# A perceiver layer on one core: products of zeros before the first rows, the identity inside x, the query weights in four pieces

## The chip, the cores and the metric

One core of a Trainium2 chip runs the whole layer in one launch. The metric is the device time of one execution in microseconds (us). The engines of the core are TensorE (PE: matmuls and transposes, with its weight loads as PEld), VectorE (DVE), ScalarE (ACT), GpSimd (POOL) and SyncE (SP), which issues every load and store. Each works through its own list of instructions in order; they wait for each other on semaphores.

## What is computed

The reference is one layer on x of 256 tokens by 512, in float32: cross-attention over 4096 context rows and the layer's own 256, then latent attention of 16 heads with rotary positions and a causal mask, then a mixture of 32 experts with one shared expert. Only the first lines matter for the change:

```python
x = x + xattn(layernorm(x), ctx_2048, ctx_2048, wq, wk, wv, wo)
# inside xattn:
q = einsum('bsd,ed->bse', x, wq)
k_new = einsum('bsd,ed->bse', x, wk)
k = concatenate([k_cache, k_new]); v = concatenate([v_cache, v_new])
attn = softmax(einsum('bqd,bkd->bqk', q, k) / sqrt(512))
out = einsum('bqk,bkd->bqd', attn, v) @ wo.T
x = x + latent_attention(layernorm(x), ...)
x = x + experts(layernorm(x), ...)
```

## The kernel before

**Precision.** Every product is made of three matmuls: each operand is split into a high part rounded to `fp32r` and a low part that holds the rest, and `product` (L375) issues high*high, low*high (or high*low) and the other cross term (L377, L380, L381). ScalarE makes the high part of a weight tile (`split_hi`, L269) and VectorE the low part (`split_lo`, L276). A result in a PSUM bank is split in the same way on its way out: `out_hi`, `out_lo` (L284, L288) and, for transposed tokens, `tokens_hi`, `tokens_lo` (L315, L319).

**Weight tiles.** Weights and context come through two slots of `raw`, `w_hi`, `w_lo`, used in turn. A tile of the first part of the kernel is 128 partitions by 2048 floats, 1 MB, in two halves of 512 KB. A half covers two chunks of 128 rows of the contraction (`x_chunk`). `load` (L330) issues both halves; except for the first two tiles it waits until the tile before in the same slot has been split (`lo_split`). The tiles follow each other: query weights (T_WQ), key weights (T_WK), eight context tiles (T_CT), value weights, eight context tiles again, and so on.

**The start, engine by engine.** SP issues (L338 to L344): the two halves of x (128 tokens each, 256 KB, into `res`), the identity (the first 128 columns of `small`, read as 128 rows of 512 B), the query weights in two halves, the rest of `small` (mask, rotary tables, router weights, gains: 640 KB), the key weights in two halves, the rope weights. VectorE takes the statistics of each half of x, GpSimd the power -0.5 (`root`), VectorE normalizes to `xn`. TensorE waits for the identity (L441), transposes `xn`, half 0 into banks 0 and 1 and half 1 into banks 4 and 5, and then runs `project_t` (L404) twice: for each of four blocks m of output features it goes through all four chunks c of the contraction. Query results fill banks 2 and 3, key results banks 4 and 5. Then come the score groups (`score_group`, L448), each on one context tile: 24 matmuls with 512 columns.

ScalarE's list at the start (L846 to L866): high part of query half 0, the four evictions of transposed tokens, query half 1, key halves 0 and 1, two query evictions, the halves of the first context tile, two key evictions, then the constants (`ident_r`, two blocks of `mask_r`, `rw_hi`), two blocks of rope weights, and then the loop over context tiles from the second one on. VectorE (L1109 to L1130) makes the low parts in the same order.

`mask_r` has three blocks of 128 columns. Block 0 is all zeros, set by GpSimd (`mask_zeroed`); it is part of the causal mask that enters the scores of the latent attention in the middle of the kernel.

Of the kernel before, what the change touches and what calls it, by code (L numbers as in the profile page):

```python
# [29 lines left out]
F32 = mybir.dt.float32  # L30
# [5 lines left out]
P = 128  # L36
# [34 lines left out]
C_ID, C_MASK, C_COS, C_SIN, C_RW, C_BIAS, C_GQ, C_GKV, C_TIE = 0, 128, 256, 512, 768, 896, 960, 1152, 1280  # L71
# [39 lines left out]
def perceiver_layer(nc, x, small, wq, wk, wv, wo, ctx_t, ctx_n, w_qkv, w_rope, w_mla, w_exp, out):  # L111
    with ExitStack() as ctx:
# [12 lines left out]
        res = sb("res", [P, 2, D])  # L125
# [92 lines left out]
        ident_loaded = sem("ident_loaded")  # L218
# [64 lines left out]

        def out_hi(act, b, full, hi, n, rows=slice(0, P), at=0, scale=1.0):  # L284
            act.wait_ge(bank_full[b], full)
            act.activation(hi, bank[b][rows, at:at + n], ACT.Copy, scale=scale).then_inc(ev_hi, 1)  # L286
# [42 lines left out]
        def _(sp):  # L329
# [8 lines left out]
            for h in range(2):  # L338
                sp.dma_start(res[:, h, :], x[:, h, :]).then_inc(x_loaded[h], 16)
            sp.dma_start(smalls[:, C_ID:C_MASK], small[:, C_ID:C_MASK]).then_inc(ident_loaded, 16)  # L340
            load(Tile(0, T_WQ), wq, X_SIZES, first=True)
            sp.dma_start(smalls[:, C_MASK:C_END], small[:, C_MASK:C_END]).then_inc(small_loaded, 16)
            load(Tile(0, T_WK), wk, X_SIZES, first=True)
            sp.dma_start(probs[0:QR2].rearrange("p a b c -> p (a b c)"), w_rope[0:QR2, :]).then_inc(rope_w_loaded, 16)  # L344
# [27 lines left out]
        def _(pe):  # L372
            ident = smalls[:, C_ID:C_ID + P]
# [67 lines left out]
            pe.wait_ge(ident_loaded, 16)  # L441
            for h in range(2):
                transpose_half(xn, h, 4 * h, xn_ready, h + 1)
            project_t(Tile(0, T_WQ), 2, split=V_LN1 + 2)
# [145 lines left out]
            pe.wait_ge(mask_zeroed, 1)  # L590
# [254 lines left out]
        def _(act):  # L845
            split_hi(act, Tile(0, T_WQ), 0, X_SIZES, first=True)  # L846
            for h in range(2):
                tokens_hi(act, 4 * h, (F01 if h == 0 else F45)["ln1"], xt_hi, h)
            split_hi(act, Tile(0, T_WQ), 1, X_SIZES, first=True)
# [8 lines left out]
            act.wait_ge(ident_loaded, 16)  # L858
            act.copy(ident_r[:, :], smalls[:, C_ID:C_ID + P]).then_inc(consts_rounded, 1)
# [212 lines left out]
        def _(dve):  # L1072
# [41 lines left out]
            split_lo(dve, Tile(0, T_WQ), 0, X_SIZES)  # L1114
            for h in range(2):
                tokens_lo(dve, 4 * h, V_LN1 + 2 * h, xt_hi, xt_lo, h)
            split_lo(dve, Tile(0, T_WQ), 1, X_SIZES)
# [414 lines left out]
        def _(pool):  # L1532
# [5 lines left out]

            pool.memset(power[:, :], -0.5).then_inc(power_set, 1)
            pool.memset(mask_r.bitcast(F32)[:, 0, :], 0.0).then_inc(mask_zeroed, 1)  # L1540
# [91 lines left out]
```

## Time and profile before

| | |
|---|---|
| median of 3 runs | 560.92 us (560.76 to 561.14) |
| the profiled execution, its own time | 559.95 us |
| its span, first to last instruction | 558.2 us |
| TensorE busy | 534.0 us, 96% |
| VectorE busy | 392.9 us, 70% |
| ScalarE busy | 314.0 us, 56% |
| mean granted TensorE clock | 0.997 |
| DMA | 86.43 MB, mean 155 GB/s |

All times in the rows are microseconds from the start of the span. Busy shares are averages over stages with different limits; a stage is read by the wait that ends last in it. A name such as L279 is the line of the helper that issued the instruction, so one line stands for many places: the time and the tile tell them apart.

### The profile page before, as it was taken

What the parts mean: (1) busy time and instruction counts of PE and PEld (TensorE: products, weight loads), DVE (VectorE), ACT (ScalarE), POOL (GpSimd) and SP (SyncE); (2) the same over time, 40 slices, a digit from 0 to 9 for tenths busy, and PEclk for the clock granted to TensorE, in tenths of its full rate; (3) what the DMA queues carried; (4) which work ended last, traced back from release to release, by engine and by line L of the source; (5) the groups of instructions that cost most, each with busy time, mean ns of one, the idle gap of its engine ahead of it and who ended that gap; (6) DMA issues with size and microseconds to landing.
All of it is one profiled execution on the core that took longest, in us unless ns stands there. A gap on an engine that the chain in (4) does not pass through costs nothing.

```text
span 558.2 us, 9698 instructions
## 1 busy us (share of the span) xinstructions
PE 534.0 (96%) x3448; PEld 478.8 (86%) x3448; DVE 392.9 (70%) x597; ACT 314.0 (56%) x506; POOL 5.4 (1%) x14
## 2 busy tenths in 40 slices
PE   3999999999888999998999999999999999999997
PEld 3978888888778888877889999999999999999996
DVE  4686655557877777677587767767767777677675
ACT  3666476753566676765645464564654655645631
POOL 1000000000100000000000000000000000000000
PEclk9999999999998999999999999999999999999999
DMA  8855534445132222440636456455465464564621
GB/s 263 256 179 200 175 128 136 161 155 170 38 113 77 77 75 75 128 174 11 228 114 225 155 183 210 149 205 188 155 220 170 168 220 149 195 205 144 215 66 39
DMA packets 19138, 86.43 MB, mean 155 GB/s; under 512 B 2128, under 2 KB 2256, under 8 KB 19024
## 3 DMA queue, kind: packets, MB, share of 16 engines
q1 hardware_dynamic: 19120, 86.19, 46.4%
q8 instruction: 11, 0.18, 0.1%
q14 instruction: 7, 0.06, 0.0%
HBM read 85.66 MB, written 0.52 MB: 154 GB/s over the span
## 4 chain that ended last, share of the span: by engine, by line
PE 80%; DVE 8%; ACT 7%; issue 2%; DMA 1%; SPq 0%; ACTq 0%; POOL 0%; DVEq 0%
PE bank L377 26%; PE bank L381 26%; PE bank L380 26%; ACT scores L960 2%; DVE w_lo L279 2%; ACT scores L969 2%; ACT w_hi L274 1%; DVE m_neg L1299 1%; PE bank L486 1%; DMA raw<-wq_dram 1%; ACT operands L286 1%; DVE operands L290 1%; PE bank L640 1%; DVE res L1449 1%; DVE rope_w L1129 0%
## 5 line engine op out<-in xcount | busy, mean ns | idle before, releaser
L274 ACT CAST w_hi<-raw 128x1024 fp32r<-128x1024 f32 (+1 forms) x160 | 161.7, 1044 | 138.6 <-PE bank L377 122.0
L279 DVE TENSOR_TENSOR w_lo<-raw,w_hi 128x1024 fp32r<-128x1024 f32 (+1 forms) x160 | 187.9, 1215 | 12.2 <-ACT w_hi L274 10.3
L377 PE MATMUL bank<-xt_hi,w_hi 128*128 128x256 f32 x544 | 155.2, 285 | 2.9 <-DVE xt_lo L311 2.9
L380 PE MATMUL bank<-xt_lo,w_hi 128*128 128x256 f32 x544 | 154.6, 284 | 0.0
L381 PE MATMUL bank<-xt_hi,w_lo 128*128 128x256 f32 x544 | 154.5, 284 | 0.0
L377 PE MATMUL bank<-w_hi,operands 128*128 128x512 f32 (+1 forms) x320 | 126.4, 395 | 3.1 <-DVE operands L311 1.4
L381 PE MATMUL bank<-w_hi,operands 128*128 128x512 f32 (+1 forms) x320 | 124.5, 389 | 0.0
L380 PE MATMUL bank<-w_lo,operands 128*128 128x512 f32 (+1 forms) x320 | 124.5, 389 | 0.0
L377 PEld LDWEIGHTS bank<-xt_hi,w_hi 128*128 128x128 f32 x544 | 104.9, 193 | 4.8 <-issue 3.3
L380 PEld LDWEIGHTS bank<-xt_lo,w_hi 128*128 128x128 f32 x544 | 105.0, 193 | 1.5
L381 PEld LDWEIGHTS bank<-xt_hi,w_lo 128*128 128x128 f32 x544 | 105.0, 193 | 0.0
L377 PEld LDWEIGHTS bank<-w_hi,operands 128*128 128x128 f32 x320 | 60.2, 188 | 15.5 <-DVE operands L311 1.8
L1449 DVE SCALAR_TENSOR_TENSOR res<-bank,weights,res 128x512 f32<-128x512 f32 x68 | 50.8, 750 | 30.0 <-PE bank L381 30.0
L381 PEld LDWEIGHTS bank<-w_hi,operands 128*128 128x128 f32 x320 | 60.0, 187 | 13.8
L380 PEld LDWEIGHTS bank<-w_lo,operands 128*128 128x128 f32 x320 | 60.1, 188 | 11.1
L290 DVE TENSOR_TENSOR operands<-bank,operands 128x512 fp32r<-128x512 f32 (+2 forms) x81 | 47.4, 626 | 28.8 <-ACT operands L286 28.7
L286 ACT ACTIVATE operands<-bank 128x512 fp32r<-128x512 f32 (+2 forms) x81 | 40.3, 560 | 32.6 <-PE bank L381 17.3
L1511 DVE TENSOR_TENSOR operands<-scores,operands 128x512 fp32r<-128x512 f32 x32 | 22.2, 693 | 41.1 <-ACT operands L1058 41.1
L377 PE MATMUL bank<-operands 128*128 128x256 f32 (+2 forms) x110 | 31.4, 285 | 1.8 <-DVE operands L290 1.8
L381 PE MATMUL bank<-operands 128*128 128x256 f32 (+2 forms) x110 | 31.7, 288 | 0.0
L380 PE MATMUL bank<-operands 128*128 128x256 f32 (+2 forms) x110 | 31.7, 288 | 0.0
L377 PEld LDWEIGHTS bank<-operands 128*128 128x128 f32 x110 | 21.6, 196 | 5.2 <-DVE operands L290 5.0
(152 smaller groups left out, 503.2 us busy)
## 6 DMA issues: line engine op xcount, KB each, us to landing
raw<-w_exp_dram SPq DMA_DIRECT2D x34, 896.0 KB, 4.8
raw<-w_exp_dram SPq DMA_DIRECT2D x34, 640.0 KB, 5.6
raw<-ctx_t_dram SPq DMA_DIRECT2D x16, 512.0 KB, 4.4
raw<-ctx_n_dram SPq DMA_DIRECT2D x16, 512.0 KB, 3.8
raw<-w_mla_dram SPq DMA_DIRECT2D x16, 512.0 KB, 4.2
raw<-wq_dram SPq DMA_DIRECT2D x2, 512.0 KB, 6.4
raw<-wk_dram SPq DMA_DIRECT2D x2, 512.0 KB, 11.5
raw<-wv_dram SPq DMA_DIRECT2D x2, 512.0 KB, 4.6
```

Of the source, the lines that this page charges most:

```text
L274: act.copy(w_hi[:, t.slot, at:at + n], raw[:, t.slot, at:at + n]).then_inc(hi_split[k], 1)
L279: eng.tensor_tensor(w_lo[:, t.slot, at:at + n], raw[:, t.slot, at:at + n], w_hi[:, t.slot, at:at + n].bitcast(F32), ALU.subtract) \
L286: act.activation(hi, bank[b][rows, at:at + n], ACT.Copy, scale=scale).then_inc(ev_hi, 1)
L290: dve.tensor_tensor(lo, bank[b][rows, at:at + n], hi.bitcast(F32), ALU.subtract) \
L377: ins = pe.matmul(o, a[0], b[0], start=start, stop=False)
L380: pe.matmul(o, a[0], b[1], start=False, stop=False)
L381: return pe.matmul(o, a[1], b[0], start=False, stop=stop)
L486: ins = pe.transpose(bank[2 * ring + h][:, k * P:k * P + P], probs[:, ring, h, k * P:k * P + P], ident)
L960: act.activation(pair_probs[:, hd, at:at + n], bank[2 + hd][:, at:at + n], ACT.Exp, bias=m_bias[:, k:k + 1], scale=q_scale[:, h:h + 1], ac ...
L969: act.activation(v, v, ACT.Copy, scale=m_inv[:, 2 * hd + h:2 * hd + h + 1]).then_inc(m_norm, 1)
L1449: dve.scalar_tensor_tensor(out=res[:, h, :], in0=bank[b][:, :], scalar=w, in1=res[:, h, :], op0=ALU.mult, op1=ALU.add).then_inc(res_done, 1)
L1511: dve.tensor_tensor(h_lo[:, s % 2, :], h_row[:, s % 2, :], h_hi[:, s % 2, :].bitcast(F32), ALU.subtract).then_inc(ev_lo, 1)
```

## The change

1. GpSimd zeroes block 0 of `mask_r` before it sets `power`. TensorE waits for that alone and issues 12 matmuls of this block with itself (128 x 128 by four repeats of the block, 512 columns) into bank 7, and one each into banks 2 and 3, which leaves zeros there. Two more follow the transposes of half 0 and four those of half 1.
2. x comes from the host as one array of 128 by 1280: half 0, identity, half 1, and 128 unused columns. The first transfer brings half 0 and the identity (rows of 2560 B, 320 KB), the second half 1 (256 KB). `res` and `ident` are views of `first_rows`. `small` loses its identity columns and is loaded whole, behind the key weights.
3. The query weights come in four transfers of 256 KB, one for each chunk, with a semaphore each, and are split chunk by chunk (`wq_hi`, `wq_lo`). ScalarE rounds chunk 0 and chunk 1 before the evictions of half 0 and half 1 of the tokens, VectorE takes chunk 0 before the tokens and chunks 1 to 3 after them.
4. `project_q` turns the two loops of `project_t` around: for each chunk c all four blocks m. All results accumulate onto the zeros in banks 2 and 3 (`start=False`).

```diff
-        res = sb("res", [P, 2, D])
+        first_rows = sb("first_rows", [P, 2 * (D + P)])
+        res = first_rows[:, :].rearrange("p (h n) -> p h n", h=2)[:, :, 0:D]
+        ident = first_rows[:, D:D + P]
...
+        def wq_hi(act, c):
+            k, at = c // 2, OFF[c // 2] + (c % 2) * 512
+            act.wait_ge((loaded_b if k else loaded_a)[0] if c % 2 else wq_loaded[k], 16)
+            act.copy(w_hi[:, 0, at:at + 512], raw[:, 0, at:at + 512]) \
+               .then_inc(hi_split[k] if c % 2 else wq_hi_split, 1)
+
+        def wq_lo(dve, c):
+            k, at = c // 2, OFF[c // 2] + (c % 2) * 512
+            if c % 2:
+                dve.wait_ge(hi_split[k], 1)
+            else:
+                dve.wait_ge(wq_hi_split, k + 1)
+            dve.tensor_tensor(w_lo[:, 0, at:at + 512], raw[:, 0, at:at + 512],
+                              w_hi[:, 0, at:at + 512].bitcast(F32), ALU.subtract) \
+               .then_inc(lo_split[k] if c % 2 else wq_lo_split, 1)
...
-            for h in range(2):
-                sp.dma_start(res[:, h, :], x[:, h, :]).then_inc(x_loaded[h], 16)
-            sp.dma_start(smalls[:, C_ID:C_MASK], small[:, C_ID:C_MASK]).then_inc(ident_loaded, 16)
-            load(Tile(0, T_WQ), wq, X_SIZES, first=True)
-            sp.dma_start(smalls[:, C_MASK:C_END], small[:, C_MASK:C_END]).then_inc(small_loaded, 16)
+            for h, (at, n) in enumerate(((0, D + P), (D + P, D))):
+                sp.dma_start(first_rows[:, at:at + n], x[:, at:at + n]).then_inc(x_loaded[h], 16)
+            for c in range(NC):
+                at = OFF[c // 2] + (c % 2) * 512
+                part = (loaded_b if c // 2 else loaded_a)[0] if c % 2 else wq_loaded[c // 2]
+                sp.dma_start(raw[:, 0, at:at + 512], wq[:, c * 512:c * 512 + 512]).then_inc(part, 16)
             load(Tile(0, T_WK), wk, X_SIZES, first=True)
+            sp.dma_start(smalls[:, :], small[:, :]).then_inc(small_loaded, 16)
...
-            pe.wait_ge(ident_loaded, 16)
+            def zeros(b, stop):
+
+                pe.matmul(bank[b][:, :].rearrange("p (a b) -> p a b", a=4), mask_r[:, 0, :],
+                          mask_r[:, 0:1, :].broadcast_to([P, 4, P]), start=True, stop=stop)
+
+            def project_q():
+
+                for c in range(NC):
+                    if c % 2:
+                        ready(Tile(0, T_WQ), c // 2)
+                    else:
+                        pe.wait_ge(wq_lo_split, c // 2 + 1)
+                        pe.wait_ge(ev_lo, V_LN1 + 2 + c // 2)
+                    for m in range(NC):
+                        ins = product(bank[2 + m // 2][:, (m % 2) * T:(m % 2) * T + T],
+                                      x_chunk(Tile(0, T_WQ), c, m * P, P), (xt_hi[:, c, :], xt_lo[:, c, :]),
+                                      False, c == NC - 1 and m % 2 == 1)
+                        if c == 1 and m == NC - 1:
+                            ins.then_inc(used[0], 1)
+                        if c == NC - 1 and m % 2:
+                            ins.then_inc(bank_full[2 + m // 2], 1)
+
+            pe.wait_ge(mask_zeroed, 1)
+            for _ in range(12):
+                zeros(7, True)
+            for b in (2, 3):
+                zeros(b, False)
+            pe.wait_ge(x_loaded[0], 16)
             for h in range(2):
                 transpose_half(xn, h, 4 * h, xn_ready, h + 1)
-            project_t(Tile(0, T_WQ), 2, split=V_LN1 + 2)
+                for _ in range(2 + 2 * h):
+                    zeros(7, True)
+            project_q()
...
-            split_hi(act, Tile(0, T_WQ), 0, X_SIZES, first=True)
-            for h in range(2):
-                tokens_hi(act, 4 * h, (F01 if h == 0 else F45)["ln1"], xt_hi, h)
-            split_hi(act, Tile(0, T_WQ), 1, X_SIZES, first=True)
+            wq_hi(act, 0)
+            tokens_hi(act, 0, F01["ln1"], xt_hi, 0)
+            wq_hi(act, 1)
+            tokens_hi(act, 4, F45["ln1"], xt_hi, 1)
+            wq_hi(act, 2)
+            wq_hi(act, 3)
...
-            split_lo(dve, Tile(0, T_WQ), 0, X_SIZES)
+            wq_lo(dve, 0)
             for h in range(2):
                 tokens_lo(dve, 4 * h, V_LN1 + 2 * h, xt_hi, xt_lo, h)
-            split_lo(dve, Tile(0, T_WQ), 1, X_SIZES)
+            for c in range(1, NC):
+                wq_lo(dve, c)
...
+            pool.memset(mask_r.bitcast(F32)[:, 0, :], 0.0).then_inc(mask_zeroed, 1)
             pool.memset(power[:, :], -0.5).then_inc(power_set, 1)
-            pool.memset(mask_r.bitcast(F32)[:, 0, :], 0.0).then_inc(mask_zeroed, 1)
```

## Rows read from the trace of the kernel before

**Rows 1.** The page: busy time by engine; the chain that ended last, by engine.
```profile
PE 534.0 (96%) x3448; PEld 478.8 (86%) x3448; DVE 392.9 (70%) x597; ACT 314.0 (56%) x506; POOL 5.4 (1%) x14
...
PE 80%; DVE 8%; ACT 7%; issue 2%; DMA 1%; SPq 0%; ACTq 0%; POOL 0%; DVEq 0%
```

**Rows 2.** Waits of TensorE, whole span: total us, times, longest.
```profile
PE bank L377 <- DVE xt_lo L311: 5.8, 3, 2.9
```

**Rows 3.** Timeline, 0 to 12: start, duration, engine, line, operation, [idle before, releaser].
```profile
0.78 0.20 POOL L1540 MEMSET mask_r<- 128x128 f32 x1
...
2.13 0.91 SPq L336 DMA_DIRECT2D raw<-wq_dram  x2
...
5.40 0.54 DVE L1093 TENSOR_SCALAR xn<-res,mean_var,rstd 128x512 f32<-128x512 f32 x1
...
6.08 2.01 PE L397 MATMUL bank<-smalls,xn 128*128 128x128 f32 x8 [6.08 <-DMA smalls<-small_dram]
6.38 0.55 DVE L1093 TENSOR_SCALAR xn<-res,mean_var,rstd 128x512 f32<-128x512 f32 x1 [0.45 <-POOL rstd L1536]
...
7.59 1.04 ACT L274 CAST w_hi<-raw 128x1024 fp32r<-128x1024 f32 x1 [5.56 <-DMA raw<-wq_dram]
8.54 1.20 ACT L306 ACTIVATE xt_hi<-bank 128x256 fp32r<-128x256 f32 x4
8.66 1.23 DVE L279 TENSOR_TENSOR w_lo<-raw,w_hi 128x1024 fp32r<-128x1024 f32 x1 [1.73 <-ACT w_hi L274]
9.80 1.41 DVE L311 TENSOR_TENSOR xt_lo<-bank,xt_hi 128x256 fp32r<-128x256 f32 x4
...
11.03 0.55 PE L377 MATMUL bank<-xt_hi,w_hi 128*128 128x256 f32 x1 [2.94 <-DVE xt_lo L311]
```

**Rows 4.** Busy time of TensorE by stretch: length, busy (matmuls), granted clock, DMA, GB/s.
```profile
11.00:15.30 4.30, 4.27 (x19) 1.00 1.04 276
15.70:24.50 8.80, 8.80 (x76) 1.00 0.82 262
```

**Rows 5.** Timeline, 20 to 31.
```profile
20.58 1.05 ACT L274 CAST w_hi<-raw 128x1024 fp32r<-128x1024 f32 x1 [0.88 <-DMA raw<-ctx_t_dram]
...
21.66 2.50 DVE L279 TENSOR_TENSOR w_lo<-raw,w_hi 128x1024 fp32r<-128x1024 f32 x2 [1.24 <-ACT w_hi L274]
...
21.85 1.05 ACT L274 CAST w_hi<-raw 128x1024 fp32r<-128x1024 f32 x1 [0.22 <-DMA raw<-ctx_t_dram]
...
24.66 0.39 PE L377 MATMUL bank<-w_hi,operands 128*128 128x512 f32 x1
...
24.86 0.60 ACT L286 ACTIVATE operands<-bank 128x512 fp32r<-128x512 f32 x1 [1.46 <-PE bank L381]
24.89 0.40 PE L380 MATMUL bank<-w_lo,operands 128*128 128x512 f32 x1
...
25.35 0.29 ACT L859 CAST ident_r<-smalls 128x128 fp32r<-128x128 f32 x1
...
30.77 0.50 PE L377 MATMUL bank<-w_hi,operands 128*128 128x512 f32 x1 [0.35 <-DVE w_lo L279]
```

**Rows 6.** DMA by stretch: length, granted TensorE clock, DMA busy share, GB/s.
```profile
2.00:3.50 1.50, 1.00 0.93 333
3.50:5.50 2.00, 1.00 0.75 130
5.50:10.00 4.50, 1.00 1.00 368
```

**Rows 7.** Waits of TensorE from 36 to 140: total us, times, longest.
```profile
PE bank L377 <- DVE operands L290: 0.4, 1, 0.4
```

**Rows 8.** Busy time of TensorE by stretch, around 170: columns as in rows 4.
```profile
165.00:169.00 4.00, 1.44 (x9) 1.00 0.43 169
...
170.00:171.00 1.00, 1.00 (x6) 0.50 0.00 0
```

More of the change, by code:

```diff
@@ L68 @@
 E_SIZES = (1280, 1024, 768)
-C_ID, C_MASK, C_COS, C_SIN, C_RW, C_BIAS, C_GQ, C_GKV, C_TIE = 0, 128, 256, 512, 768, 896, 960, 1152, 1280
+C_MASK, C_COS, C_SIN, C_RW, C_BIAS, C_GQ, C_GKV, C_TIE = 0, 128, 384, 640, 768, 832, 1024, 1152
 C_END = C_TIE + 2 * GROUPS * GROUPS
@@ L217, in perceiver_layer @@
         x_loaded = [sem(f"x_loaded{h}") for h in range(2)]
-        ident_loaded = sem("ident_loaded")
+        wq_loaded = [sem(f"wq_loaded{k}") for k in range(2)]
+        wq_hi_split = sem("wq_hi_split")
+        wq_lo_split = sem("wq_lo_split")
         small_loaded = sem("small_loaded")
@@ L372, in _ @@
         def _(pe):
-            ident = smalls[:, C_ID:C_ID + P]
             def product(o, a, b, start, stop, told=None):
@@ L589, in _ @@
             rope_queries(1, midway=lambda: transpose_kv(1))
-            pe.wait_ge(mask_zeroed, 1)
             pe.wait_ge(consts_rounded, 4)
@@ L857, in _ @@
                 out_hi(act, 4 + b, F45["k"], flat(k_hi[:, 2 * b:2 * b + 2, :]), 512)
-            act.wait_ge(ident_loaded, 16)
-            act.copy(ident_r[:, :], smalls[:, C_ID:C_ID + P]).then_inc(consts_rounded, 1)
+            act.copy(ident_r[:, :], ident).then_inc(consts_rounded, 1)
             act.wait_ge(small_loaded, 16)
@@ L1568 @@
     a = {k: np.asarray(v) for k, v in inputs.items()}
-    rows = a["x"][0].reshape(2, P, D).transpose(1, 0, 2)
+    rows = np.zeros((P, 2, D + P), np.float32)
+    rows[:, :, 0:D] = a["x"][0].reshape(2, P, D).transpose(1, 0, 2)
+    rows[:, 0, D:D + P] = np.eye(P, dtype=np.float32)
     small = np.zeros((P, C_END), np.float32)
-    small[:, C_ID:C_ID + P] = np.eye(P, dtype=np.float32)
     small[:, C_MASK:C_MASK + P] = np.triu(np.full((P, P), MASKED, np.float32), 1)
@@ L1619 @@
     arrays = {
-        "x": rows, "small": small,
+        "x": rows.reshape(P, 2 * (D + P)), "small": small,
         "wq": _chunked(a["L0_xattn_wq"].T), "wk": _chunked(a["L0_xattn_wk"].T),
```

## The prediction, made before the changed kernel ran

> **What bounds the kernel now.** I read the page first: TensorE is busy for 96% of the span and carries 80% of the chain that ended last [rows 1]. A kernel like that gets shorter only where TensorE stands still or runs slowly. The list of TensorE's waits over the whole span then says that the largest stall on data is at the start: the longest single one of the three waits for `xt_lo` is the 2.9 us before the first product [rows 2, 3]. The timeline of the first 12 us shows the rest: eight transposes from 6.08 to 8.09, nothing until 11.03, and then the matmuls of 256 columns [rows 3]. Two stretches laid side by side show how these run: 19 of them fill 4.27 us up to 15.3, 0.22 each, and 76 fill 8.80 us after 15.7, 0.12 each [rows 4]. So the array works at the lower of its two clock levels (1.2 GHz) for the first 4.5 us of the projection and at 2.4 GHz afterwards, although the granted clock in these rows reads 1.00 in both; the price of one matmul is what shows the step. The query and key projections have 96 matmuls; at 0.12 they would take 11.5 us, and they took 24.66 - 11.03 = 13.6 us [rows 3, 5]. So 2.1 us is the price of the low clock, and everything before 11.03 is the price of getting going.
>
> What sets 11.03? ScalarE waits for 512 KB of query weights until 7.59, rounds them (1.04), only then evicts the transposed tokens (8.54 to 9.74); VectorE takes 1.23 for `w_lo` and then about 0.35 for each `xt_lo`, and TensorE needs three of them [rows 3].
>
> **Part by part: getting to the first product.** (a) The memset of `mask_r` at 0.78 [rows 3] comes first on GpSimd now, so the zeros can start at about 1.0. It delays `power` by 0.2 us, which is read only after 4.6, so nothing waits. (b) Fourteen matmuls of 512 columns (twelve to bank 7, one each to banks 2 and 3). At twice the cold price of 256 columns each is 0.44, 6.2 in all, ending at 7.2; if the clock rises 4.5 us after they begin, as it did after 11.03, the last three or four cost 0.235 (24.66 to 24.89 [rows 5]) and they end at about 6.3. No row shows a matmul whose moving operand repeats one block four times; the nearest are these 512-column ones and I take their price. (c) The first half of x brings the identity: 64 KB more, 0.17 us at 368 GB/s [rows 6]. The normalized halves, ready at 5.94 and 6.93 before [rows 3], are ready at about 6.1 and 7.1. The transposes of half 0 begin at 6.3 instead of 6.08 and half 1 at 7.15; two zeros between them and four behind cost 0.5 and 0.9 warm and end at 8.6, before the products can begin. (d) ScalarE now waits for 256 KB of weights, not 512. They stand 64 KB and a slower identity transfer earlier in the queue, so I put them at 5.2 to 6.0, rounded (half of 1.04) before the transposes are done. Then: evictions of half 0 at 7.0 to 7.6 (0.3 each), second piece 7.6 to 8.1, half 1 from 8.1, first at 8.4. VectorE: `w_lo` of 512 columns 0.6 (half of 1.23) from 7.1, two `xt_lo`, and the third ends at 8.8. First product at 8.9 instead of 11.03: 2.1 us earlier. (e) The chunk order has the same 48 products, the waits for pieces 1 to 3 come 1.4 us apart (12 matmuls of 0.12), and VectorE delivers a piece in 0.6, so none of them stalls. Both query banks are full only at the end, 14.6; their evictions are needed at about 21, so that costs nothing. The key weights, 512 KB apiece, now stand ahead of the 640 KB of small constants and land before they are needed at 14.6.
>
> So queries and keys are done at 8.9 + 11.5 = 20.4, 4.2 us earlier than 24.66.
>
> **Not all of it arrives.** What is late next is the first context tile. Its halves landed at 20.58 and 21.85, and ScalarE waited for both [rows 5]: `w_lo` of half a was ready at 22.9, only 1.8 us before it was used. So the question is how much earlier the DMA queue delivers it. The bytes ahead of it are the same (the identity moved, nothing was dropped). The engines moved 333 GB/s while x came, then 130 GB/s from 3.5 to 5.5 at a busy share of 0.75, and 368 afterwards [rows 6]. That dip lies where the identity is read in rows of 512 B, cut out of longer rows; it is short of 2.0 x (368 - 130) = 476 KB, or 1.3 us. In the changed kernel the identity is part of rows of 2.5 KB. Bounds of this gain: 0 (the dip is how a queue starts on weights) and 1.3. I take 1.0, nearer the upper end, since x itself came at full rate just before in rows of 2 KB. SP issues four pieces instead of two, 0.45 each (2.13, 0.91 for two [rows 3]), but it loses the identity's issue ahead of them, so the key weights are issued no later than before.
>
> The Trainium skill, in DMA: Bandwidth & Descriptors (Specifications), says that transfers reach line rate from 512 B upwards. By that rule the identity's rows are not slow and this term is 0, which gives the lower bound below; the same page (its rule on batching) favours transfers of 1 MiB and would rather see the four pieces as a loss. Against this the two halves of x, 256 KB each, came at 333 GB/s.
>
> **The second gate.** ScalarE's order is: context half b, two key evictions, then the constants (from 25.35), the rope weights, and the next context tile, whose `w_lo` TensorE waited for, 0.35 us, until 30.77 [rows 5]. Before, the second key eviction at 24.86 waited for TensorE, 1.46 us. Now it waits for nothing: half b lands at 21.85 - 1.0 = 20.85, is rounded until 21.9, two evictions at 0.5 apart follow, and the constants begin at 22.9. That is 25.35 - 22.9 = 2.45 us earlier, and the whole chain of fixed work behind it (constants, rope weights, `w_lo` at 30.77) moves with it. The constants' own transfer, moved behind the key weights, is still ahead of the context tile in the same queue and so has landed by 20. The first score group starts at about 21.9 and takes 5.8, so TensorE still waits for the second tile: it starts at 30.77 - 2.45 = 28.3. With the DMA bounds, half b at 21.85 gives constants at 23.9 (gain 1.45), and at 20.55 gives 22.6 (gain 2.75). From 36 to 140 us the waits of TensorE add up to 0.4 us [rows 7], and each load is released by a split of an earlier tile, so the start carries through.
>
> **Sum.** Own time of the profiled execution 559.95 (span 558.2 and 1.75 around it), less 2.45 = 557.5. The median of the runs shown is 560.92, 0.97 above that execution; the same 2.45 gives 558.5. The profiled one may have had a shorter cold stretch than the others; that part of the difference is what the zeros remove, so I put 558.4.
>
> **Rivals.** (1) More than forecast: the clock later on falls into place. From 165 to 169 TensorE works 1.44 us of 4, and from 169 on the granted clock falls to 0.50 and stays there about 3.4 us (one of these microseconds is shown [rows 8]), at a price of half of that, 1.7 us. If the shifted schedule meets it differently and the drop disappears, or the dip goes entirely and the unprofiled runs were colder, the gain is 3.2 to 4.2: 556.7 to 557.7. The Trainium skill (TensorE: Matmul & The Clock Gate, Part 1) says the number of cold matmuls of one kernel changes from run to run; this trace is one execution and cannot show it, and the three runs lie within 0.4 us. (2) The same mechanism the other way: the shift turns another pause of TensorE into such a drop, 1.7 more: gain 0.75, 560.2. (3) The change does not do what it says: zeros do not raise the clock. Then 14 of them end at 7.2, eight transposes (1.8) and six more zeros (2.6) end at about 11.6, the first product starts there, 0.6 later than now, and the cold 2.1 is paid as before: 560.9 + 0.6 = 561.5. Against it: the array is used like by any other product. (4) Slower: the zeros are too dear. TensorE takes them in order ahead of all real work. There are 20, and transposes and start take 2.5 us; the key projection must end by 24.66, so the first product must start by 13.1: the point from which it decides is (13.1 - 2.5) / 20 = 0.53 us each. Were the repeated operand read at a quarter of the rate (1.7 us cold, 0.94 warm), the zeros would take some 20 us, and the first product would start about 12 us after 13.1: near 572. Nothing in the profile speaks for it, except that no such operand is there.
>
> **How the numbers follow.** Forecast 0.62 (its own range 558.1 to 559.5, gains 1.45 to 2.75 either way of the two bases), rival 1 0.14, rival 2 0.08, rival 3 0.10, rival 4 0.06. Faster by over 0.2% (1.12 us, about what a measurement of this kernel can tell from no change) means under 559.8: forecast, rival 1 and a little of rival 2, 0.80. Same: rivals 2 and 3 with edges, 0.14. Slower 0.06. The range of 8 in 10 takes in the forecast, most of rival 1 and rival 2: 556.7 to 560.3.
>
> **What will show it.** Zeros from 1.0, starting 0.44 apart and then about half that before 6.5. First product near 8.9 with starts 0.12 apart at once. The DMA rate from 3.5 to 5.5 well above 130 GB/s, and context half b landing near 20.9. TensorE's first score product near 21.9 after a wait of more than 1 us for `w_lo`, the next tile at 28.3. The prediction is wrong if the zeros keep their 0.44 throughout, if the context tile lands where it did (gain 1.45), if it lands later, or if the granted clock shows another stretch of 0.50 beyond 140 us.

## The result and the profile after

The changed kernel took 554.92 us (median of four executions, 554.8 to 555.69) against 560.84 for the kernel before (four, 560.59 to 561.14): a ratio of 0.9897, 95% interval 0.988 to 0.9914, or 5.9 us less. The forecast was 558.4 with a range from 556.7, so the gain was more than twice the one forecast (2.5) and lies outside the range. Eight more executions of the same kernel, later, had a median of 558.19 (554.65 to 558.85). Both numbers are true, and most of this part is about how they go together. One execution of the kernel before, at 905 us with a mean granted clock of 0.646, is in none of the numbers below.

The profiled execution spans 553.2 us, 5.0 less than before. The start, in the timeline of the changed kernel (start, duration, engine, line, operation, and in brackets the idle time before and what ended it):

```profile
1.00 5.97 PE L464 MATMUL bank<-mask_r 128*128 128x512 f32 x14 [1.00 <-POOL mask_r L1590]
1.67 1.85 SPq L363 DMA_DIRECT2D raw<-wq_dram  x4
...
5.39 0.62 ACT L291 CAST w_hi<-raw 128x512 fp32r<-128x512 f32 x1 [3.37 <-DMA raw<-wq_dram]
...
6.81 0.60 PE L418 MATMUL bank<-first_rows,xn 128*128 128x128 f32 x4
...
7.85 1.61 DVE L331 TENSOR_TENSOR xt_lo<-bank,xt_hi 128x256 fp32r<-128x256 f32 x4
...
8.06 1.17 PE L464 MATMUL bank<-mask_r 128*128 128x512 f32 x4
...
9.28 0.35 PE L398 MATMUL bank<-xt_hi,w_hi 128*128 128x256 f32 x1
...
9.47 0.28 PE L401 MATMUL bank<-xt_lo,w_hi 128*128 128x256 f32 x1
9.59 0.28 PE L402 MATMUL bank<-xt_hi,w_lo 128*128 128x256 f32 x1
```

The first weights are taken up at 5.39 (7.59 in [rows 3]), the first product starts at 9.28 instead of 11.03, and the products start 0.12 apart at once, the price of 2.4 GHz, where [rows 4] had 0.22. The same kernel further on, at the two gates of the prediction:

```profile
18.58 1.05 ACT L278 CAST w_hi<-raw 128x1024 fp32r<-128x1024 f32 x1 [2.68 <-DMA raw<-ctx_t_dram]
19.85 1.06 ACT L278 CAST w_hi<-raw 128x1024 fp32r<-128x1024 f32 x1 [0.23 <-DMA raw<-ctx_t_dram]
20.81 1.08 ACT L306 ACTIVATE operands<-bank 128x512 fp32r<-128x512 f32 x2
21.77 0.30 ACT L909 CAST ident_r<-first_rows 128x128 fp32r<-128x128 f32 x1
...
21.03 0.47 PE L398 MATMUL bank<-w_hi,operands 128*128 128x512 f32 x1
...
27.20 0.50 PE L398 MATMUL bank<-w_hi,operands 128*128 128x512 f32 x1 [0.32 <-DVE w_lo L283]
```

Against [rows 5], the context halves are taken up 2.0 earlier (18.58 and 19.85), the constants begin 3.58 earlier (25.35 to 21.77), and the second score group starts 3.57 earlier (30.77 to 27.20). That is the gain of the start in this pair of executions: 3.6 of 5.0. The rest is found where the prediction had put its first rival. Busy time of TensorE in the changed kernel by stretch (length, busy and count, granted clock, DMA share, GB/s), to be read beside [rows 8]:

```profile
161.00:165.00 4.00, 1.49 (x10) 1.00 0.35 128
165.00:166.00 1.00, 0.68 (x6) 1.00 0.00 0
166.00:168.00 2.00, 2.00 (x20) 1.00 0.00 0
168.00:170.00 2.00, 2.00 (x19) 1.00 0.00 0
```

The pause is there, 3.55 us earlier (the first product behind it starts at 165.32 instead of 168.87), but no stretch at 0.50 follows it.

What such a stretch costs can be read from the profiles of this kernel and of those below. From the start of the second score group to the end of the span it takes 525.9 to 526.0 us in the eight profiles without a low stretch (526.0 here), 527.3 to 527.4 in the four that have 3.4 us at 0.50 behind the pause (the kernel before is one), and 528.7 to 528.9 in the four that have 6.8 us. So a low stretch costs 1.4 or 2.8 us, and the 5.0 of this pair are 3.6 for the start and 1.4 for the stretch.

DMA of the changed kernel at the start, beside [rows 6] (the same columns):

```profile
2.00:3.50 1.50, 1.50 (x5) 1.00 0.90 299
3.50:5.50 2.00, 2.00 (x6) 1.00 0.93 290
5.50:10.00 4.50, 4.45 (x25) 1.00 0.95 301
```

The dip to 130 GB/s from 3.5 to 5.5 is gone, at the price of a lower rate after it (301 against 368). The same columns for longer stretches, the first two lines from the kernel before and the last two from the changed one:

```profile
0.00:10.00 10.00, 2.01 (x8) 1.00 0.76 245
10.00:18.00 8.00, 6.97 (x41) 1.00 1.02 260
0.00:10.00 10.00, 8.95 (x34) 1.00 0.79 244
10.00:18.00 8.00, 8.00 (x69) 1.00 1.02 315
```

By 10 us both kernels had moved the same amount, so the dip had been made up by then. The earlier landing of the context tile goes with the 0.44 MB that the changed kernel moved more between 10 and 18 us.

### The profile page after: what moved, and what is told of

The parts are those of the page before. It is cut to its first block, busy times and chain, and to the rows that moved or that the text cites. A ratio compares the mean times of both kernels' runs of the same rounds, so it can differ in the third digit from the quotient of the medians.

```text
span 553.2 us, 9743 instructions
## 1 busy us (share of the span) xinstructions
PE 537.0 (97%) x3468; PEld 480.2 (87%) x3468; DVE 392.9 (71%) x599; ACT 314.1 (57%) x508; POOL 5.4 (1%) x14
## 4 chain that ended last, share of the span: by engine, by line
PE 78%; DVE 9%; ACT 8%; issue 3%; DMA 2%; POOL 0%; ACTq 0%; DVEq 0%; SPq 0%; POOLq 0%
PE bank L398 25%; PE bank L402 25%; PE bank L401 25%; ACT scores L1010 2%; DVE w_lo L283 2%; ACT scores L1019 2%; DMA raw<-ctx_t_dram 2%; DVE m_neg L1350 1%; ACT w_hi L278 1%; PE bank L536 1%; DVE operands L310 1%; PE bank L464 1%; ACT operands L306 1%; PE bank L689 1%; DVE first_rows L1500 1%
## 5 line engine op out<-in xcount | busy, mean ns | idle before, releaser
L278 ACT CAST w_hi<-raw 128x768 fp32r<-128x768 f32 (+1 forms) x158 | 159.6, 1044 | 130.8 <-PE bank L398 122.1
L283 DVE TENSOR_TENSOR w_lo<-raw,w_hi 128x768 fp32r<-128x768 f32 (+1 forms) x158 | 185.6, 1216 | 8.3 <-ACT w_hi L278 6.3
L1500 DVE SCALAR_TENSOR_TENSOR first_rows<-bank,weights,first_rows 128x512 f32<-128x512 f32 x68 | 50.8, 751 | 30.0 <-PE bank L402 29.9
L310 DVE TENSOR_TENSOR operands<-bank,operands 128x512 fp32r<-128x512 f32 (+2 forms) x81 | 47.4, 627 | 28.4 <-ACT operands L306 28.3
L398 PE MATMUL bank<-operands 128*128 128x256 f32 (+2 forms) x110 | 30.8, 280 | 1.8 <-DVE operands L310 1.8
L401 PE MATMUL bank<-operands 128*128 128x256 f32 (+2 forms) x110 | 31.1, 283 | 0.0
L402 PE MATMUL bank<-operands 128*128 128x256 f32 (+2 forms) x110 | 31.0, 282 | 0.0
L398 PEld LDWEIGHTS bank<-operands 128*128 128x128 f32 x110 | 20.9, 190 | 5.2 <-DVE operands L310 5.0
```

The lines of the kernel that those rows point to most:

```text
L278: act.copy(w_hi[:, t.slot, at:at + n], raw[:, t.slot, at:at + n]).then_inc(hi_split[k], 1)
L283: eng.tensor_tensor(w_lo[:, t.slot, at:at + n], raw[:, t.slot, at:at + n], w_hi[:, t.slot, at:at + n].bitcast(F32), ALU.subtract) \
L310: dve.tensor_tensor(lo, bank[b][rows, at:at + n], hi.bitcast(F32), ALU.subtract) \
L398: ins = pe.matmul(o, a[0], b[0], start=start, stop=False)
L401: pe.matmul(o, a[0], b[1], start=False, stop=False)
L402: return pe.matmul(o, a[1], b[0], start=False, stop=stop)
```

## Experiments

Each kernel ran several times, beside the kernel before on the same chip. With each execution comes the mean granted clock of TensorE. In the executions that were profiled, 1.00 goes with no stretch at 0.50, 0.997 with 3.4 us of it, 0.994 with 6.8 us, and 0.999 with a fall behind the last matmul (as in the changed kernel's first profile); the other executions are read by the same key. For the later stage this turned out to be as telling as the time.

### Zeros in the later pause

```diff
 project_pair(Tile(j, T_M + s + 1), ...)
+if start:
+    for _ in range(5): zeros(0, True)
 ...
 rope_transpose(j * 2 + (s + 2))
+if start:
+    for _ in range(5): zeros(0, True)
```

> The kernel before with ten zero products in the pause of TensorE between 164.7 and 168.9 (five behind the projections of the second pair, five behind the rope transposes of the first pair step, into bank 0, which is free there). My theory: the granted clock no longer falls to 0.50 after 169, its mean is 1.00 in every run, and the time is 1.4 to 1.7 lower, 559.3. Rival (the low stretch is in the profiled execution alone, or lies off the chain): 560.8, the other runs of the kernel before showing a clock of 1.00 too.

Measured: 558.95 (558.25 to 560.04, five executions), ratio 0.9967 (0.995 to 0.9983), every execution at 0.999 or 1.00. The expectation held: 1.6 less than the kernel before (560.57 in the same job, twenty executions). Timeline of TensorE in this kernel:

```profile
165.55 1.30 PE L443 MATMUL bank<-mask_r 128*128 128x512 f32 x5
167.02 1.24 PE L645 MATMUL bank<-smalls,scores 128*128 128x128 f32 x6 [0.17 <-ACT scores L980]
...
168.23 1.41 PE L443 MATMUL bank<-mask_r 128*128 128x512 f32 x5
169.84 0.38 PE L377 MATMUL bank<-operands 128*128 128x256 f32 x1 [0.20 <-DVE operands L290]
170.07 0.28 PE L380 MATMUL bank<-operands 128*128 128x256 f32 x1
```

The zeros fit into the pause (0.17 and 0.20 are left idle), and the products behind it keep the high clock. So the low stretch is real, lies on the chain, and costs the kernel before 1.6 us in the median. The zeros cost nothing themselves: with them, too, it is 526.0 us from the second score group to the end.

> The changed kernel with the ten zero products in the pause of TensorE around 161 to 165 (the same two places as in the kernel before with zeros in its pause). My theory: the changed kernel no longer has the stretch at 0.50 behind that pause, so there is nothing left to gain: 554.9, same. Rival (zeros in the pause help for another reason than the clock, or the changed kernel still loses to the clock in executions that were not profiled): 553.2 to 553.5.

Measured: 555.78 (555.49 to 555.89), all at 1.00. That is 0.9 more than the first result of the changed kernel, not the same, and the profiled execution says where: its second context half was taken up at 20.63 instead of 19.85, and the constants began at 22.54 instead of 21.77. The time of the transfers varies by that much from execution to execution. From there on the two profiles run alike: the second score group starts at 27.96 instead of 27.20, and the spans differ by about as much, 0.7.

### Does the changed kernel keep the clock?

```diff
-for _ in range(2 + 2 * h):
+for _ in range(2 + 10 * h):
```

> The changed kernel with eight more zero products (12 instead of 4) behind the transposes of half 1: all work behind them 1.7 us later, nothing else changed, the clock high throughout the start. Theory A (the pause at 161 to 165 loses the clock or keeps it by where it falls in time): with 1.7 of shift the granted clock falls to 0.50 after the pause in some or all executions, mean clock 0.997, 558.0. Theory B (the zeros at the start, or the way the early stage runs, keep it whatever the time): no low stretch, mean clock 1.00, 556.6.

Measured: 558.0 (555.94 to 558.8), with 1.00 once, 0.997 three times and 0.994 twice. Theory B fell. The numbers of theory A came true (a loss in some or all executions, 558.0), but not the reason that it gives: the kernel kept the clock once and lost it five times with the same shift. That raised the question whether the first four executions of the changed kernel were typical, so it ran again unaltered.

> The changed kernel itself, unaltered, in more executions. Open point: its four executions so far had no stretch at 0.50 behind the pause at 161 to 165, while kernels shifted by 0.5 to 1.7 us had none, one or two from execution to execution. Theory A (the changed kernel was in luck): some executions now show mean clocks of 0.997 or 0.994 and 1.0 to 3 us more; median 555.5 to 557.5. Theory B (its schedule keeps the clock reliably): all at 0.999 or 1.00, median 554.9 to 555.8.

All executions of the changed kernel, the first four and these eight:

```
mean clock   time, us
0.999-1.00   554.65 554.80 554.82 554.90 554.95 555.69
0.997        557.93
0.991-0.994  558.10 558.28 558.63 558.65 558.85
```

Theory A held, with a median above the range that it gave (558.19 against 555.5 to 557.5). The kernel has two times, 554.9 and 558.3. Of the 3.4 between them the clock accounts for 2.8 in most cases; the rest is the start, as the next profile shows. The profile taken this time is of the second kind. Its second score group starts at 28.03 instead of 27.20, and behind the pause (the stretches as above, and two more) it reads:

```profile
161.00:165.00 4.00, 2.40 (x18) 1.00 0.58 205
165.00:166.00 1.00, 0.00 (x0) 0.97 0.00 0
166.00:168.00 2.00, 1.78 (x8) 0.50 0.00 0
168.00:170.00 2.00, 2.00 (x11) 0.50 0.00 0
170.00:172.00 2.00, 2.00 (x11) 0.50 0.00 0
172.00:174.00 2.00, 2.00 (x15) 0.81 0.40 104
```

The schedule up to there is the same within 1 us, and the granted clock is at 0.50 for almost 7 us: 11 matmuls in 2 us instead of 20. The Trainium skill (TensorE: Matmul & The Clock Gate, Part 1) says that one kernel shows different numbers of cold matmuls from run to run; these executions show that for a pause in the middle of a kernel too.

The kernel before has the same lottery with other odds: of some seventy executions beside these experiments about four in ten were at 0.994, half at 0.997, and seven at 0.999, with times from 559.0 to 562.8. At the 1.4 and 2.8 us of the profiles this mix costs 1.8 in the mean, about what zeros in the pause gave back. But the medians of the three groups are 561.1, 560.5 and 559.8, closer together than the 1.4 us for each step in the profiles; why is not known, since none of these executions was profiled.

> The changed kernel with the ten zero products in the pause once more, as the base of this comparison. Theory: the pause is the only place at which the clock is lost, so every execution shows a mean clock of 1.00 and 555.0 to 556.0, while the changed kernel alone jumped between 554.7 and 558.9. Rival (the narrow first result was luck too): some executions at 0.997 or below and 557.5 or more.

Measured: 555.81 (554.4 to 556.37), all at 0.999 or 1.00. With zeros in the pause the lottery of the clock is gone, twice. A spread of 2 us is left. The profiled execution, the slowest of them, shows it at the start: its second context half was taken up at 21.26, and its second score group starts at 28.59.

### The start, with the later stretch taken out

All kernels of this part have the ten zero products in the pause, so they compare by the start alone. The base is the kernel before with them, 558.95; the changed kernel with them is at 555.8. The difference, 3.15 us, is the estimate of what the change itself is worth; it compares kernels of different jobs, whose own executions spread by up to 2 us.

> The changed kernel without its zeros into bank 7 at the start, but with ten zero products in the pause at 165, so that the later low stretch is out of the comparison. The changed kernel with the same ten measured 555.8. Theory: the start's zeros are worth the cold stretch that they cover, 2.0 to 2.6 at the first product's stage: 558.0, clock 1.00 behind the pause. Rival (most of what the zeros gave was the later stretch): under 557.

Measured: 556.81 (556.3 to 557.2). Edit: the loops that issue zeros to bank 7 are taken out, those to banks 2 and 3 stay. The start's zeros are worth 1.0, not the expected 2.0 to 2.6, and the rival (under 557) held. The first run of this kind, without the zeros in the pause:

> The changed kernel without its 18 zero products into bank 7 (the two into banks 2 and 3 stay, the accumulation needs them). My theory: the zeros are worth the cold stretch only. The projection still starts near 9.3, its first 4 to 5 us run at 0.22 a matmul, the key projection ends near 23.0 instead of 20.9 and the constants on ScalarE begin near 23.7 instead of 21.8: 2.0 us slower than the changed kernel, 556.9. Rival (the zeros do nothing, the order of loads and chunks does it all): 554.9, starts 0.12 apart from the first product or a context tile that lands too late for the difference to matter.

Measured: 558.82, all five at 0.997, ratio 0.9964 (0.995 to 0.9979). It looked like 3.9 us for the zeros against the first result of the changed kernel, where 2.0 had been expected; 2.9 of that was the clock behind the pause (1.4) and transfers that happened to be early in that first result. ScalarE in the profile with the later zeros shows why so little is left:

```profile
20.51 1.05 ACT L278 CAST w_hi<-raw 128x1024 fp32r<-128x1024 f32 x1 [0.22 <-DMA raw<-ctx_t_dram]
21.46 0.59 ACT L306 ACTIVATE operands<-bank 128x512 fp32r<-128x512 f32 x1
23.15 0.60 ACT L306 ACTIVATE operands<-bank 128x512 fp32r<-128x512 f32 x1 [1.09 <-PE bank L402]
23.64 0.29 ACT L911 CAST ident_r<-first_rows 128x128 fp32r<-128x128 f32 x1
```

Without the zeros the keys come late and the second key eviction waits 1.09 for TensorE; with them the wait is gone, but the context half at 20.5 is then the gate and nothing more can be won.

> The kernel before with the zeros at the start alone (12, 3 and 10) and ten in the pause. Base: the kernel before with the ten alone, 558.95. Theory: with the old loads the weights come so late that TensorE stands again after its zeros, the clock can fall back during the projection (seen once, 0.50 from 12.8 on), and the context tile is the gate: 558.2 to 558.9. Rival (the zeros are worth their 2.1 us by themselves): 557.0.

Measured: 557.73 (556.57 to 558.09), 1.2 less than the base. Edit: zeros at the start (12, 3 and 10), the earlier memset and the ten in the pause, on the kernel before. The time lies between the two expectations. In the profile the first product came at 11.97, after 1.84 idle behind the zeros, and the products ran at the high clock. Without the zeros in the pause the same start had given this:

> The kernel before with zero products alone (12 ahead, 3 and 10 behind the two sets of transposes, all into bank 7; GpSimd zeroes the block first). Loads and order as before. My theory: the first product stays at 11.0, starts are 0.12 apart at once, the keys are done near 22.6, then the context tile (landed at 21.85) is the gate: constants at 23.9 instead of 25.35, gain 1.45, so 559.4. Rival (the zeros give the whole gain, with the clock later on): under 557. Rival (zeros worthless): 560.8.

Measured: 559.82 (558.44 to 562.1), from 1.00 (558.44) to 0.991 (562.10) in mean clock. Its profile shows the clock lost at the start too, after TensorE stood 1.9 us between its zeros and its first product:

```profile
12.00:14.00 2.00, 1.86 (x8) 0.61 1.06 272
14.00:16.00 2.00, 2.00 (x12) 0.53 1.03 217
...
168.00:170.00 2.00, 0.63 (x5) 0.87 0.00 0
170.00:172.00 2.00, 2.00 (x11) 0.50 0.00 0
172.00:174.00 2.00, 2.00 (x11) 0.50 0.00 0
```

So what zeros gain can be lost again when they end too early; with 1.84 and 1.89 us idle the clock was kept in one profile and lost in the other.

> The kernel before with the identity inside the rows of x and with ten zero products in the pause. The kernel before with the ten alone measured 558.95. Theory: the weights land about 0.3 us earlier in the mean and the context tile 1.2, but the keys end late (cold start) and gate everything: 558.5, gain 0.3 to 0.6. Rival (the identity's rows of 512 B cost 1.3 on the path, as the prediction had it): 557.7.

Measured: 558.07 (557.51 to 559.48), 0.9 less than the base. Edit: `first_rows` instead of `res`, the identity in the first transfer, the rest of the kernel before. That is more than expected (0.3 to 0.6) and less than the rival (1.25). The weights were taken up at 7.05 and the context tile at 19.06, but the cold keys still ended late (constants at 24.82). Alone, without the zeros in the pause:

> The kernel before with the identity inside the rows of x and nothing else. My theory: the dip of 130 GB/s from 3.5 to 5.5 was the identity's 512 B rows. The rate there is 280 or more, the query weights land 1.0 to 1.3 us earlier (ScalarE starts on them near 6.4 instead of 7.59), the first product near 9.9, still cold, and the context halves land near 19.3 and 20.5 instead of 20.58 and 21.85. Keys done near 23.5: gain 1.1 to 1.3, 559.6. Rival (rows of 512 B are at line rate, the context tile landed earlier because the small constants and pieces changed places): landing as before, gain under 0.3, 560.8.

Measured: 560.3, ratio 0.9989 (0.9978 to 1.0), well short of the 1.1 to 1.3 expected, with the rate from 3.5 to 5.5 at 226 GB/s instead of 130. In all profiles, this rate is 130 to 184 GB/s where the identity comes by itself (four) and 215 or more where it comes inside x. So its own transfer did slow the queue there. The Trainium skill (DMA: Bandwidth & Descriptors, Specifications) puts line rate at 512 B and above; here the 2 us with 64 KB in such rows went at 130 GB/s, and without them at 226. Whether the rows or the small separate transfer did it, no run tells apart. From 10 to 18 us, where the context tile gained, the rate is 260 to 285 in the four and 290 and 301 with the identity alone moved; why it is higher there stays open.

> The changed kernel with the projection block by block (each block over all four chunks) and ten zero products in the pause. Base: 555.8. Theory: TensorE stands up to 1.4 us in its first block, but the context tile's second half lands at 19.9 to 20.6 and is the gate, so only 0.3 to 0.8 of it reaches the end: 556.3. Rival (chunk order is worth its whole 1.4): 557.2.

Measured: 555.49 (555.41 to 555.78). Edit: in `project_q` the loop over m goes outside the loop over c, the waits stay. The expectation missed (556.3): block by block is as fast in the median as chunk by chunk (555.8). TensorE in this kernel:

```profile
9.63 0.28 PE L402 MATMUL bank<-xt_hi,w_lo 128*128 128x256 f32 x1
10.16 0.39 PE L398 MATMUL bank<-xt_hi,w_hi 128*128 128x256 f32 x1 [0.25 <-DVE w_lo L300]
...
10.76 0.39 PE L398 MATMUL bank<-xt_hi,w_hi 128*128 128x256 f32 x1
...
11.36 0.39 PE L398 MATMUL bank<-xt_hi,w_hi 128*128 128x256 f32 x1
```

Its first block does stand for each piece, 0.6 or more from one chunk to the next instead of 0.36, and ends about 1.1 late in all. The medians do not show it, but the profile does. Here the second context half was taken up early, at 19.08, and the second key eviction then waited 1.47 for TensorE; the constants began at 22.58, 3.5 behind that half, where it is 1.92 in the changed kernel (19.85 to 21.77). So with this order the keys were the gate, and an execution with an early context tile loses up to about 1 us by it (an estimate: the keys end at 21.9 here and at 20.9 there); with a late tile it loses nothing. Without the zeros in the pause the same edit:

> The changed kernel with the four pieces of weights as they are, but the query projection goes block by block again (all four chunks for the first block of outputs), so the first block waits for the last piece to be split at 11.3. Theory: TensorE stands 1.6 us in the first block; queries and keys are done near 22.5 instead of 20.9, constants begin near 23.0 instead of 21.8: 1.2 to 1.6 slower, 556.3, more if the shift brings the low stretch back (then 557.8). Rival (the context tile gates anyway): 554.9.

Measured: 558.21 (556.96 to 559.17), at 0.997 twice and 0.994 six times. It is near the second number of the expectation (557.8), but the unaltered kernel has the same low stretches and 558.19, so the order is not what brought them. In its profile, too, the second key eviction waits for TensorE, 0.35.

> The changed kernel with the small constants loaded ahead of the key weights again, as before. The key weights land 1.8 us later (near 12 and 13.4), needed at 15.0. Theory: no matter for the time, the first context half still lands near 18.5: 554.9. Rival (the place of the constants is what brought the context tile 2 us forward): it lands near 19.3 or later, TensorE waits for it, 555.7 or more.

Measured: 557.12 (555.6 to 559.83), mean clocks from 1.00 to 0.991; the one execution at 1.00 took 555.6. Edit: the load of `smalls` ahead of the key weights. The context halves came as in the changed kernel (18.57, 19.86), so the place of the constants is not what brought the tile forward, and the rival fell; but the second half of the key weights came at 14.55, not 13.4, TensorE waited for it, and the constants began at 22.75 instead of 21.77. So the place of the constants is worth up to 1 us, by the key weights. With the mixed clocks this is read from the profile, not from the median.

### Two versions meant to be better

> A version meant to beat both. The changed kernel with ten zero products in the pause, the small constants and the rope weights loaded behind the first context tile, and the splits of constants and rope weights ahead of the key evictions on ScalarE and VectorE. Theory: the first context tile lands near 15 instead of 18.5, scores start right behind the keys at 20.9, the second tile is ready before the first score group ends at 26.6, so both waits of TensorE for w_lo (0.3 to 1.1 us) are gone: 0.7 to 1.2 less than the changed kernel with zeros in the pause (555.8), so 554.6 to 555.1, and a narrower spread. Rival (the rope weights land too late and hold ScalarE): same or slower.

Measured: 559.48 (555.37 to 561.57). The rival held. ScalarE and the wait of TensorE in it:

```profile
18.06 1.05 ACT L278 CAST w_hi<-raw 128x1024 fp32r<-128x1024 f32 x1 [1.50 <-DMA raw<-ctx_t_dram]
19.01 0.29 ACT L915 CAST ident_r<-first_rows 128x128 fp32r<-128x128 f32 x1
21.13 0.50 ACT L918 CAST mask_r<-smalls 128x128 fp32r<-128x128 f32 x2 [1.83 <-DMA smalls<-small_dram]
...
24.52 1.99 ACT L922 CAST rope_w<-probs 96x1024 fp32r<-96x1024 f32 x2 [2.69 <-DMA probs<-w_rope_dram]
```

```profile
PE bank L400 <- DVE w_lo L283: 4.0, 1, 4.0
```

The rope weights, issued at 11.86, landed only at 24.5; they shared the queue with the tiles behind them. From 11.86 to 24.5 the DMA moved 3.5 MB, and the rope weights with all that was issued ahead of them and had not landed come to 2.5 MB at most. ScalarE, in order, held the second context tile back, TensorE waited 4.0 us for it, and the clock fell behind that wait (0.84 and then 0.50 from 31 on in the profile; a mean below 0.999 in ten of twelve executions).

> The changed kernel with ten zero products in the pause, and with the four small copies of constants (0.8 us on ScalarE, the router's low part on VectorE) moved from behind the key evictions to behind the query evictions, where ScalarE waits 2.6 us for the context tile; loads as in the changed kernel. Theory: rope weights and the second context tile are split 0.8 earlier, TensorE's second wait for w_lo (0.3 to 0.6) is gone: 0.5 less than the same without the move, 555.1 to 555.3. Rival (that wait is hidden): same.

```diff
 for b in range(2): out_hi(act, 2 + b, F23["q"], ...)
+act.copy(ident_r ...); act.wait_ge(small_loaded, 16); act.copy(mask_r ...) x2; act.copy(rw_hi ...)
 for k in range(2): split_hi(act, Tile(0, T_CT), k, X_SIZES)
 for b in range(2): out_hi(act, 4 + b, F45["k"], ...)
-act.copy(ident_r ...); act.wait_ge(small_loaded, 16); act.copy(mask_r ...) x2; act.copy(rw_hi ...)
 act.wait_ge(rope_w_loaded, 16)
```

Measured: 555.22 (554.07 to 555.53), all at 1.00, ratio to the kernel before 0.9906 (0.989 to 0.9921). In the profile the copies sit at 15.70 to 16.6, in ScalarE's wait, the rope weights begin at 21.46, and TensorE's wait for the second context tile is gone from its list. It is 0.6 below the changed kernel with zeros in the pause, about what was expected; with ranges that overlap I call that likely, not shown. It is faster than the kernel before, and than the changed kernel in the typical case (the twelve executions of that have a median of 556.8).

## Why the prediction was wrong

**The bound and the place: right.** The start was the place to win, the first product and the two gates (context tile, then constants and rope weights) were named, and in the profile after, TensorE waits 0.32 for `w_lo` at the second gate as said. The first product came at 9.28 (8.9 forecast); the zeros ended at 6.8, not 6.3, because the clock rose later. At the first gate the sign did not come: the first score product started at 21.03, right behind the keys, where 21.9 and a wait of more than 1 us were forecast.

**The DMA term: near in size, wrong in its reason.** Forecast 1.0 with an upper bound of 1.3, measured 2.0 for both halves of the context tile in the profiled pair. But the landing varies: in executions with the same loads the second half was taken up at 19.1, 19.85, 20.6 and 21.3, and 20.85 was forecast. The second score group was forecast for 28.3; in the four profiles of the changed kernel, with and without zeros in the pause, it started at 27.20, 28.03, 27.96 and 28.59. The reason given was the dip, and that had been made up by 10 us; the gain came between 10 and 18 us, for which the prediction had no term.

**The base: the profiled execution of before was an early one.** Its constants began at 25.35; in the kernel with zeros in the pause, which is the same up to there, they began at 26.32. The prediction took the 0.97 between that execution and the median of before into its base and counted 0.1 of it as a gain of the zeros. Cleared of the later stretch, the change is worth 3.15 us (558.95 to 555.8), against the 2.45 forecast and above its bound of 2.75.

**The step that failed: the low stretch behind the pause was taken as fixed.** The forecast carried it over unchanged and gave 0.14 to its absence, priced at 1.7 (it costs 1.4), and the best case with all else going well was a gain of 4.2. In the kernel before, 3.4 or 6.8 us at 0.50 are there nine times in ten; the first four executions of the changed kernel had none. The measured 5.9 is then 3.15 for the start, 1.9 for the stretches that the kernel before pays (560.84 against 558.95 with zeros in the pause), and 0.9 that four executions at 554.9 have over the cleared 555.8. For the last part the profiles give early transfers (the second score group at 27.20 against 27.96 and 28.59), which is luck. Against the forecast of 2.5, then, 1.9 of the missing 3.4 is the stretch, 0.9 luck with the transfers, and 0.6 to 0.7 the size of the start. In the eight later executions six had the stretches again, and the median was 558.19, close to the forecast; this is in part luck too, since most of them had 6.8 us at 0.50 where the forecast had carried over 3.4. So the prediction had the mechanism as a rival, but treated something that differs from execution to execution as a property of the schedule. A range that took it in would have had two humps, 554.5 to 556 and 557.5 to 559.

**Rivals and sums.** The slower one (dear zeros) fell: the 14 zeros took 5.97 us, 0.43 each, as priced by the nearest rows. Zeros do raise the clock, so that the change does not do what it says fell too. The rival of another drop came true in a form of its own in the later executions: not a second pause, but twice the length behind the same one. The forecast's own range is given as 558.1 to 559.5 for both bases; from the profiled base its gains give 557.2 to 558.5, so the range as written fits the median alone. Of the parts, two are worth about 1 us each beside the others (the start's zeros, the loads with the identity inside x), the place of the constants up to 1, and the chunk order nothing in the medians and up to about 1 in an execution with an early context tile.

**What stays open.** Why the changed kernel kept the clock in its first four executions and lost it in six of the next eight, and whether its odds differ from those of the kernel before, is not settled by twelve executions. The time of the pause alone does not decide it: by the fixed 526 us behind it and the 1.75 around the span, the execution of the delayed kernel that kept the clock (555.94) started its second score group near 28.2, an estimate, and the profiled ones that lost it at 28.03 and 28.33. Why the context tile lands up to 2.2 us apart with the same loads is open as well.

## What to carry to other kernels

Look at the granted clock of every execution before comparing medians: a pause of a few microseconds in the middle of a kernel can cost 1.4 or 2.8 us behind it in one execution and nothing in the next, and a change elsewhere can seem to win or lose that much. Cheap products on zeros that fill such a pause (free bank, operands at hand) took this out in all executions of the seven kernels that had them there and no longer wait elsewhere, though 1 to 2 us of spread from the loads is left. They are the first thing to add before other changes are measured. At a start that is bound by loads, speed on TensorE is worth only what the next tile's landing leaves of it; ask for each gain which transfer will be the gate then.

## What the hardware showed that was not expected

- The granted clock behind the same pause was 1.00 in some executions and 0.50 for 3.4 or 6.8 us in others, at a price of 1.4 and 2.8 us, with a schedule that was the same within 1 us before it (two profiles of the changed kernel, above).
- The granted clock reads 1.00 at a start where the distance between matmuls (0.22 instead of 0.12 for 256 columns) shows the low level, [rows 4].
- Transfers issued later take bandwidth from earlier ones: 768 KB of rope weights landed 12.6 us after their issue when they stood behind one context tile; at most 2.5 MB were outstanding up to them, and the DMA moved 3.5 MB in that time. In the changed kernel, ahead of the context tile, they took 12.5.
